# The softmax's subtraction of the maximum: 18 GpSimd instructions an image, or 6 adding DMA transfers on GpSimd's queue

## The reference, cut to what matters

```python
a = x_pool @ W_a + b_a
a = a.reshape(b, h * w, HEADS, KK, KK).transpose(0, 2, 1, 3, 4)
a = jax.nn.softmax(a * scale, axis=-1)
out = jnp.einsum('bnpqk,bnpkd->bnpqd', a, v_un)
...
folded = folded.at[:, ii[...], jj[...], :].add(out)
x = x + _L0_conv_ref(_gn(x), ...)
x = x + _L1_conv_ref(_gn(x), L1_conv_w)
```

## Time and profile before

| | before |
|---|---|
| median of 3 runs (range) | 5119.74 us (5117.42 to 5121.8) |
| span of the profiled execution | 5120.9 us |
| VectorE busy | 4730.3 us (92%) |
| TensorE matmul busy | 4119.3 us (80%), granted clock 0.85 |
| GpSimd busy | 4037.2 us (79%) |
| ScalarE busy | 2005.6 us (39%) |
| 16 DMA engines, mean share | 13.0% and 2.5% in two queues |

### The profile page before, as it was taken

One profiled execution on the slowest core, in us unless ns is written; L12 is line 12 of the kernel. 1 busy time (PEld: TensorE's weight loads), 2 busy tenths in 40 slices (PEclk: granted clock), 3 DMA queues, 4 the chain that ended last, 5 costly groups with the idle time before them and its releaser, 6 DMA issues.

```text
span 5120.9 us, 55367 instructions
## 1 busy us (share of the span) xinstructions
PE 4119.3 (80%) x13632; PEld 2114.1 (41%) x13632; DVE 4730.3 (92%) x3723; ACT 2005.6 (39%) x2753; POOL 4037.2 (79%) x3628
## 2 busy tenths in 40 slices
PE   4877887878887888878788887888878888878885
PEld 2434444434444344444344443444434444434442
DVE  5799999999999999999999999999999999999997
ACT  4424444334443344432444433444324444334431
POOL 5787877877877888778878788787787787887883
PEclk7988888888888788888888888888888888888887
DMA  1110111101111111111011111111110111111111
GB/s 39 38 38 24 47 44 37 47 21 40 47 33 47 36 25 47 42 39 47 21 40 47 33 47 30 31 47 38 43 47 15 46 47 33 47 24 37 47 29 28
DMA packets 126083, 194.36 MB, mean 38 GB/s; under 512 B 14248, under 2 KB 115464, under 8 KB 122472
## 3 DMA queue, kind: packets, MB, share of 16 engines
q1 hardware_dynamic: 97384, 155.50, 13.0%
q10 hardware_dynamic: 28672, 38.55, 2.5%
HBM read 39.22 MB, written 38.54 MB: 15 GB/s over the span
## 4 chain that ended last, share of the span: by engine, by line
POOL 45%; issue 25%; PE 18%; ACT 5%; DVE 5%; DMA 1%; SPq 0%; DVEq 0%; POOLq 0%; ACTq 0%; PEldq 0%; PEld 0%
POOL prod L363 15%; POOL part L356 10%; POOL att L351 10%; PE acc L753 10%; POOL att L345 6%; PE bc L733 4%; DVE prod L600 2%; ACT X L440 2%; POOL pc L332 2%; PE side L698 2%; ACT X L523 2%; PE side L692 1%; DVE ACC L647 1%; PE side L710 1%; DVE top L631 1%
## 5 line engine op out<-in xcount | busy, mean ns | idle before, releaser
L753 PE MATMUL acc<-prod,wo 96*96 96x392 f32 x5312 | 2478.5, 573 | 161.8 <-POOL prod L363 155.7
L600 DVE TENSOR_TENSOR prod<-bc,VAL 96x784 f32<-96x784 f32 x2048 | 1928.2, 959 | 307.5 <-PE bc L733 289.4
L363 POOL TENSOR_TENSOR prod<-prod 96x392 f32<-96x392 f32 x1440 | 1685.5, 1178 | 501.3 <-DVE prod L600 491.7
L733 PE MATMUL bc<-stack,sel 96*96 96x392 f16 x4608 | 1303.2, 378 | 633.5 <-DVE prod L600 611.5
L647 DVE SCALAR_TENSOR_TENSOR ACC<-XP,sg,ACC 96x1064 f32<-96x1064 f32 (+1 forms) x768 | 1736.2, 2281 | 14.9 <-ACT ACC L534 13.8
L753 PEld LDWEIGHTS acc<-prod,wo 96*96 96x96 f32 x5312 | 982.1, 188 | 675.1 <-issue 271.6
L733 PEld LDWEIGHTS bc<-stack,sel 96*96 96x96 f16 x4608 | 576.2, 137 | 1571.4 <-DVE prod L600 972.2
L351 POOL TENSOR_TENSOR att<-att,top 108x420 f32<-108x420 f32 (+1 forms) x576 | 750.3, 1321 | 38.3 <-ACT top L467 38.3
L345 POOL TENSOR_TENSOR att<-att,top 108x420 f32<-108x420 f32 (+1 forms) x576 | 645.1, 1138 | 144.2 <-DVE top L623 144.2
L356 POOL TENSOR_TENSOR part<-att,part 108x420 f16<-108x420 f32 (+1 forms) x576 | 737.3, 1298 | 0.0
L433 ACT ACTIVATE att<-side,ba 108x420 f32<-108x420 f32 (+1 forms) x576 | 340.5, 597 | 671.6 <-PE side L698 659.0
(11 more groups left out here) (55 smaller groups left out, 2183.7 us busy)
## 6 DMA issues: line engine op xcount, KB each, us to landing
stack<-part SPq DMA_DIRECT2D x192, 275.3 KB
stack<-part SPq DMA_DIRECT2D x192, 256.9 KB
tok_in<-in_x SPq DMA_DIRECT2D x32, 1176.0 KB, 9.7
out<-tok_out ACTq DMA_DIRECT2D x224, 168.0 KB, 4.2
stack<-part SPq DMA_DIRECT2D x192, 30.5 KB
stack<-part SPq DMA_DIRECT2D x192, 28.5 KB
X<-in_L_conv_W_a SPq DMA_DIRECT2D x1, 364.5 KB
ACC<-select SPq DMA_DIRECT2D x1, 144.0 KB
```

The lines of the kernel that those rows point to most:

```text
L363: nc.gpsimd.tensor_tensor(p[:, 0, :], p[:, 0, :], p[:, 1, :], ALU.add).then_inc(pre_added, 1)
L600: nc.vector.tensor_tensor(prod[:, g % PRODUCTS, :, :].rearrange("c a (i j) -> c a i j", j=WIN), b, v, ALU.mult).then_inc(prod_ready, 1)
L733: last = nc.tensor.matmul(bc[g % 2][0:CH, a, 0:UNIT], sel[:, which, :], stack[h][:, qi, ki * TAPS + kj, si:si + HALF, sj:sj + WIN], start= ...
L753: last = nc.tensor.matmul(acc[c % 2][0:CH, 0:UNIT], wo[:, :], prod[:, g % PRODUCTS, a, :], start=first, stop=s == LAST[c] and (g in PRE or ...
```

## The change

The nine SUB instructions of a half are replaced by three DMA transfers, issued on GpSimd's queue, that add into `att[h]`. Each covers three k-slices: destination 108 partitions by 3 x 420 (or 3 x 392) numbers, source `top[h]` read three times over with a step of zero. The reduction L623 writes the maximum negated, so that adding it subtracts. Each transfer has a semaphore of its own (`subbed[h][n]`), for which EXP n waits instead of GpSimd's `fine_step`. The first transfer of a half waits for the maximum as the first SUB did, and one more semaphore increment stands behind that wait. The table keeps the first three of the nine entries: 26, 27, 28 and 58, 59, 59.

```diff
-    SUB: ((26, 27, 28, 29, 30, 30, 32, 33, 34), (58, 59, 59, 62, 64, 64, 64, 65, 66)),
+    SUB: ((26, 27, 28), (58, 59, 59)),
...
-FINE = pieces(SUB, MUL, LOW)
+SUBS = pieces(SUB)
+FINE = pieces(MUL, LOW)
...
+        max_seen = sem("max_seen")
+        subbed = [[sem(f"subbed{h}{n}") for n in range(3)] for h in range(2)]
...
             def fine(home, what, h, k):
-                if what == SUB:
-                    if k == 0:
-                        until(pool, soft_step, done(SOFT, home, MAX, h, 3))
-                    nc.gpsimd.tensor_tensor(att[h][:, k, :], att[h][:, k, :], top[h][:, :],
-                                            ALU.subtract).then_inc(fine_step, 1)
-                elif what == MUL:
+                if what == MUL:
...
+            def subtract(home, h, n):
+                if n == 0:
+                    until(pool, soft_step, done(SOFT, home, MAX, h, 3))
+                    pool.sem_inc(max_seen, 1)
+                a, t = att[h][:, 3 * n:3 * n + 3, :], top[h][:, :]
+                t3 = bass.AP(t.tensor, t.offset, [t.ap[0], [0, 3], t.ap[1]])
+                nc.gpsimd.dma_start(a, t3, accum_op=ALU.add).then_inc(subbed[h][n], 16)
...
+                    for at, late, _, h, n in SUBS:
+                        if at == g:
+                            if s2 if late else s1:
+                                subtract(i - late, h, n)
...
             def smooth(home, what, h, n):
                 if what == EXP:
                     a = att[h][:, 3 * n:3 * n + 3, :]
-                    until(act, fine_step, done(FINE, home, SUB, h, 3 * n + 2))
+                    until(act, subbed[h][n], upto(16, home, 16))
...
-                    ins = nc.vector.tensor_reduce(top[h][:, c], by_window[:, c, :], AX.X, ALU.max)
+                    ins = nc.vector.tensor_reduce(top[h][:, c], by_window[:, c, :], AX.X, ALU.max, negate=True)
```

## The result

The changed kernel takes 5431.01 us (median of 4 runs, 5426.22 to 5444.86) against 5120.71 us before: 1.061 times the time, 95% interval 1.060 to 1.063, or 310 us more, 9.7 us an image. The forecast was 5050 us in a range of 4965 to 5265: the kernel moved the other way, and out of the range. The profiled execution's span is 5443.1 us.

A forecast was written before the change was run, and what follows sets the result against it. VectorE, nearly full and partly waiting for GpSimd, was taken as the bound. Per image 3.4 gained, 0 lost issuing, 1.2 lost landing: 2.2 us, times 32 images 70 us, so 5050 us from 5120.9, range 4965 to 5265.

The forecast's parts named there:

- What bounds the kernel: VectorE nearly full, partly held by GpSimd's SBUF reads; in the second half no engine full, the order of waits decides.
- The gain, 3.4 us an image: First half: six VectorE taps freed from the SUBs beside them; bounds 2.4 and 4.9 us; second half 0.
- worth its full size: First half: VectorE is full, so the 3.4 us an image counts whole, 32 x 3.4 = 109 us.
- nothing is lost at t = 2.0: At 2.0 us per issue, pre-adds behind GpSimd's block still finish in time for TensorE; loss 0.
- Issuing, t = 2.0: GpSimd takes 2.0 us to issue each transfer, between 0.8 and 3.5; a half's block of three takes 6.0.
- rival of the long issues: Slower: t = 3.5 makes GpSimd's block long, 5233 to 5271 us; decides from about t = 2.9; chance 0.20.
- Landing, 1.2 us: Second half: EXPs wait for transfers to land, 1.2 us lost an image, out of 0 to 4.1; first half 0.
- nearer the plain rate: Second half's landing loss chosen near plain moving, 2.7 us a transfer, where transfer 2 lands 12.0 us after the block's start.
- doubled rate: Reading the destination too doubles an add's moving to 5.4 us; second half's last lands at 21.5 us, 5.1 late.
- The rival of the late landing: Slower: doubled rate plus image load ahead make EXP 2 10.6 us late; 5319 us; chance 0.20.
- The signs of being wrong: Prediction fails if descriptor generation shuts out VectorE's taps, t is above 2.9, or adds run below half the plain rate.
- The profile's signs: Six taps about 9.3 us; second-half EXPs idle 1 to 2 us, 5 or more meaning late landing; VectorE's waits up 40.

The follow-up runs named there:

- Cutting it alone: Changed kernel with the second half's three EXPs moved from steps 64, 65, 67 to 66, 68, 69, behind the accumulator's start: 5257.11 us.
- plain copies: Changed kernel with the same transfers as copies instead of adds, so the weights are wrong: 5316.83 us, 1.038 times the kernel before.
- version with all moves: Changed kernel, image load early, second half's EXPs and SUMs later, first half's transfers at steps 26, 29, 29 and SUMs later: 5092.03 us.
- fastest version: First half by adding transfers at steps 26, 29, 29 with SUMs at 38, 39, 39, 40, second half by GpSimd instructions: 5041.97 us.

## Why the prediction was wrong, step by step

- **What bounds the kernel.** Right in what it used: the taps' busy time holds waiting for GpSimd, and the second half is ruled by the order of waits.
- **The gain, 3.4 us an image.** The size was right for the six taps: without the subtraction they fall by 3.6. That VectorE is full, so that this is "worth its full size", was not: the other 18 taps gave 45 of 115 us back, and 83 us were gained. The step that failed with the transfers is "nothing is lost at t = 2.0". I priced the block of issues by which product waits for which pre-add, and not by where the pre-add behind it would lie against a tap: tap 30 was held 2.0 us an image. The rest went to the other taps (35 us over all images) and to the landing (28 us of waiting at the SUMs), which in the first half I had at 0. Net, the first half was worth 0 and not 109 us.
- **Issuing, t = 2.0.** One issue takes 1.94 us, but the three overlap, 4.23 us for a block against the 6.0 that I took. The rival of the long issues did not happen: beside the second half's block VectorE's products wait 0.99 and 2.35 us for TensorE, and 0.99 and 2.62 at the same place before.
- **Landing, 1.2 us.** This is the step that turned the sign: the second half cost 286 us, 8.9 an image. It failed in two places. The first is the path. I priced EXP 2 against the first SUM. What cost was EXP 0 and EXP 1, 6.58 and 3.28 us, since the start of the accumulator (L498 before, L508 here) stands directly behind EXP 1, and TensorE's in-order stream behind that. The prediction had this chain behind EXP 2, and did not follow who waits for it. Cutting it alone gave 174 us, more than any other move.
- **The room on the DMA engines.** The second place. I chose "nearer the plain rate, since the DMA engines are mostly idle". The mean share says nothing of the 16 us in which image load, `stack` copies and adds meet, and the kernel before showed 0.72 to 0.86 there. An add takes 1.8 times the engine time of a copy, near the doubled rate that I had as the upper bound, but the choice of the rate did not decide the sign: at the plain rate I had the landing in time and no loss, and plain copies lose 194 us.
- **The rival of the late landing** had the doubled rate and the load, but my path: it gave 5319 us, and the range ended at 5265, below it, though it had a chance of 0.20. Its condition, an add at over 1.9 times the plain moving time, was not met either (1.8).
- **The signs of being wrong.** None of the three that I named came true: descriptors did not shut out the taps, t was not above 2.9, and the add ran at more than half the plain rate. They asked for the price of each new piece and not for who stands behind it. The profile's signs did tell: six taps at 11.10 us and not 9.3, 6.58 us before an EXP, and 334 us more of the products' waits and not 40.
- **Open.** In the version with all moves the second half still costs 50 us. VectorE's SUMs wait 95.8 us for the EXPs there and 23.8 in the fastest version; whether that is the landing (15.0 us) or the moved EXPs and SUMs themselves was not tried apart. Nor was it shown which part of a GpSimd instruction holds the tap while a transfer ahead of it is unfinished; that it is held, and that moving it cures it, is shown. It is also open why the other 18 taps take longer when the six take less, and what the lower clock alone costs.

## What to carry to other kernels

A transfer in place of an instruction is hidden only if every instruction behind its waiter can wait too: list what stands behind the wait on its engine, and then who waits for those in order, before pricing the transfer itself. Judge the room on the DMA engines in the few us in which the transfers land, not by their mean share, and count an add as nearly two copies. And when work is taken off an engine that holds up another, the gain depends on where the instructions that remain fall: here the same removal was worth 0 or 1.1% by the step at which two issues were placed, and 1.5% with the SUMs moved too.

## What was not expected of the hardware

- Three transfers issued one behind another from GpSimd's queue overlap: 4.23 us for three of 1.4 to 2.5 us.
- Generating descriptors did not hold VectorE's taps (1.30 and 1.31 us beside it), but a pre-add behind them did (3.29 us; 2.57 where two pre-adds began after the block). The Trainium skill (SBUF — State Buffer, section "Who interferes with whom") infers the first, of a `tensor_tensor`; these runs show it for a `scalar_tensor_tensor` with both inputs in SBUF.
- An add of 108 rows by 3 x 420 numbers was 448 packets, the copy of the same bytes 160. By the fixed 2.0 us and bytes / 436e3 of the Trainium skill (DMA: Bandwidth & Descriptors, section "Anatomy of one DMA — SWDGE (gpsimd) path") such a transfer would land after 3.2 us, an estimate for one transfer by itself. The traces differ: with three in flight in the quiet half the soonest plain copy of a block landed after 5.0 to 5.2 us (blocks from 1622.04 and 2116.82 on) and the soonest add after 8.1 (block from 1667.10 on); the medians over the run are 7.5 and 13.1.
